# A decoder of two layers on one core: the slot order of the first stage, and the last step of the expert tiles

## The reference, cut to what matters

```python
x = x + L0_attn(layernorm(x))            # q, k, v each projected and layer-normed; softmax(k q^T) v, plus its own input
x = x + layernorm(x) * decayed_sum(ctx * ctx)     # r = 0.9 r + ctx^2 along the tokens
x = x + L0_ffn(layernorm(x))             # 8 experts, one per token, 1024 places each; tokens past that pass through
x = x + L1_attn(layernorm(x))            # 16 heads of 16
x = x + L1_xattn(layernorm(x), ctx)
x = x + L1_ffn(layernorm(x))             # the best 2 of 8 experts, weighted by their scores
```

## Time and profile before

| | before |
|---|---|
| median of 3 runs | 2639.61 us (2637.99 to 2640.75) |
| profiled execution: its own time | 2664.65 us |
| its span, first to last instruction | 2662.7 us |
| busy share of the span | PE 87%, PEld 69%, DVE 69%, ACT 60%, POOL 52% |
| first stage | 0 to about 540 us |
| experts of the last line | about 2357 us to the end |

### The profile page before, as it was taken

One profiled execution on the slowest core, in us unless ns is written; L12 is line 12 of the kernel. 1 busy time (PEld: TensorE's weight loads), 2 busy tenths in 40 slices (PEclk: granted clock), 3 DMA queues, 4 the chain that ended last, 5 costly groups with the idle time before them and its releaser, 6 DMA issues. The chain is left out here.

```text
span 2662.7 us, 49468 instructions
## 1 busy us (share of the span) xinstructions
PE 2303.4 (87%) x16108; PEld 1840.5 (69%) x16108; DVE 1840.6 (69%) x4594; ACT 1590.2 (60%) x3199; POOL 1377.3 (52%) x1384
## 2 busy tenths in 40 slices
PE   4888888659999957999999999988699999869987
PEld 4777777549988944565656565655588777659987
DVE  4777777645665536777777777775377777679877
ACT  4878778534655425676667676776244444348765
POOL 4777777544444245455445454541266666535554
PEclk9999999869999978999999999999799999879998
DMA  2222221162333110111111111111133333247574
GB/s 64 75 64 80 64 80 57 52 178 92 104 109 110 41 32 20 41 41 41 39 42 38 43 40 42 39 34 37 44 107 130 123 125 120 105 163 241 160 213 119
DMA packets 190220, 222.78 MB, mean 84 GB/s; under 512 B 36306, under 2 KB 166879, under 8 KB 189841
## 3 DMA queue, kind: packets, MB, share of 16 engines
q1 hardware_dynamic: 165008, 163.26, 20.8%
q0 software_dynamic: 23872, 56.37, 5.9%
q10 hardware_dynamic: 1088, 0.00, 0.0%
HBM read 128.15 MB, written 90.69 MB: 82 GB/s over the span
## 5 line engine op out<-in xcount | busy, mean ns | idle before, releaser
L1592 DVE TENSOR_REDUCE f_nm<-f_raw 128x4 f32<-128x1024 f32 x256 | 312.7, 1221 | 108.8 <-PE f_raw L1705 106.0
L1428 POOL TENSOR_TENSOR f_hm<-f_hm,f_mhalf 128x64 f32<-128x64 f32 x32 | 366.4, 11449 | 2.7
L1497 ACT ACTIVATE f_PT<-f_sco 128x1024 f32<-128x1024 f32 x256 | 262.3, 1025 | 96.4 <-PE f_sco L1722 96.2
L957 ACT ACTIVATE b_hT<-b_H,b_b1r 128x512 f32<-128x512 f32 x128 | 88.4, 691 | 162.6 <-PE b_H L1087 147.2
L1722 PE MATMUL f_sco<-f_q4T,f_k4T 64*128 64x256 f32 x1024 | 130.2, 334 | 49.8 <-DMA f_q4T<-f_nmT 35.6
L1102 PE MATMUL b_O<-b_w2l,b_hTh 128*128 128x256 f32 x512 | 144.9, 283 | 0.0
L1102 PE MATMUL b_O<-b_w2h,b_hTl 128*128 128x256 f32 x512 | 144.8, 283 | 0.0
L1102 PE MATMUL b_O<-b_w2h,b_hTh 128*128 128x256 f32 x512 | 144.7, 283 | 0.0
L910 POOL DMA_INDIRECT x_scratch<-b_y,b_idx x64 | 69.6, 1088 | 143.3 <-DVE b_y L1034 127.5
L1722 PEld LDWEIGHTS f_sco<-f_q4T,f_k4T 64*128 64x128 f32 x1024 | 81.9, 197 | 84.8 <-DMA f_q4T<-f_nmT 42.6
L1705 PE MATMUL f_raw<-f_k4T,f_q4T 64*128 64x256 f32 x1024 | 130.1, 334 | 7.3 <-DVE f_nm L1592 5.7
(11 more groups left out here) (406 smaller groups left out, 7905.3 us busy)
## 6 DMA issues: line engine op xcount, KB each, us to landing
x_scratch<-a_x SPq DMA_DIRECT2D x64, 256.0 KB, 2.2
b_w<-in_L_ffn_W_dram SPq DMA_DIRECT2D x16, 1024.0 KB
d_xs<-first_in SPq DMA_DIRECT2D x24, 544.0 KB
a_x<-in_x_dram SPq DMA_DIRECT2D x32, 256.0 KB
a_cx<-in_ctx_dram SPq DMA_DIRECT2D x32, 256.0 KB
f_x<-x_scratch SPq DMA_DIRECT2D x32, 256.0 KB
f_q4T<-f_nmT SPq DMA_DIRECT2D x128, 64.0 KB
f_xr<-x_scratch SPq DMA_DIRECT2D x32, 256.0 KB
```

The source lines that it names most:

```text
L957: s.activation(hT[f % 4][:, :], HB[f % 4][:, :], ACT.Gelu, bias=b1r[:, e, f:f + 1], scale=RATIO).then_inc(hidden, 1)
L1428: g.tensor_tensor(hm[b % 2][:, :], hm[b % 2][:, :], mhalf[:, :], ALU.pow).then_inc(hroot, 1)
L1497: s.activation(PT[n % 3][:, t, :, :], heads(SCO), ACT.Exp, scale=float(DH) ** -0.5).then_inc(probs_ready, 1)
L1592: v.tensor_reduce(nm[:, t, g * HG:(g + 1) * HG], heads(RAW), AX.X, ALU.max, negate=True)\
```

## The change

In the first stage `ORDER` is written anew. The squares of the context move from step "x2" (the first part of a slot) to step "sco" (behind the transposition "in T"), one slot sooner for a given row. The parts "in qk1" and "ln kT" change places. "pre stats" moves ahead of "sco inv" and "sco att", and "sco stats" moves to the end of the slot, behind "in v". In the experts `finish` runs two tiles late through nearly all of the second class (one tile late in four tiles near the end, and not late in the last four), where before it did so in the first four tiles of that class. The comparisons of `hide_seen` are done for all tiles at once before the first tile, and `load_part` takes the row number that the load of the same tile left in a register.

```diff
         ORDER = (
-            "x2 kv", "in norm", "route logits", "sco scores", "ln sq", "in T", "in low", "x2 sums", "x2 add",
-            "x2 stats", "sco exp", "route ranks", "in qk0", "ln scale", "sco prT", "ln kT", "in qk1", "x2 norm",
-            "sco inv", "sco att", "ln qT", "x2 T", "sco stats", "pre stats", "x2 pass", "in v")
+            "in norm", "route logits", "sco scores", "ln sq", "in T", "in low", "sco kv", "x2 sums", "x2 add",
+            "x2 stats", "sco exp", "route ranks", "in qk0", "ln scale", "sco prT", "in qk1", "ln kT", "x2 norm",
+            "pre stats", "sco inv", "sco att", "ln qT", "x2 T", "x2 pass", "in v", "sco stats")
...
-                   "sco exp": exps, "sco prT": take_prT, "x2 kv": square_ctx, "x2 norm": norm4, "x2 T": take_x2nT, "x2 pass": passed_by})
+                   "sco exp": exps, "sco prT": take_prT, "sco kv": square_ctx, "x2 norm": norm4, "x2 T": take_x2nT, "x2 pass": passed_by})
...
-        place, mask = sb("place", [P, T]), [sb(f"mask{n}", [P, T]) for n in range(ZR)]
+        place, hide = sb("place", [P, T]), [sb(f"hide{k}", [P, HALF - ex.WHOLE, T]) for k in range(2)]
...
-                ex.load_tile(sync, m)
+                row = ex.load_tile(sync, m)
+                if m >= HALF:
+                    row_of[m] = row
...
             def load_part(m):
-                row = sync.value_load(ex.row[0:1, m:m + 1], min_val=0, max_val=ex.spare)
+                row = row_of.pop(m)
...
             def hide_seen(m):
                 k = of_class(m)
-                if m == ex.WHOLE:
-                    dve.wait_ge(consts, 3)
-                n = m % HALF - ex.WHOLE
+                dve.wait_ge(masked, 2)
                 dve.wait_ge(scattered[(m - ZR) % XR], 16 * T * (turn(m - ZR) + 1))
-                v.tensor_scalar(mask[m % ZR][:, :], place[:, :], ex.over[k][:, n:n + 1], float(ex.OUT_OF_RANGE), ALU.is_lt, ALU.mult)\
-                    .then_inc(masked, 1)
-                masks[0] += 1
-                dve.wait_ge(masked, masks[0])
-                v.tensor_tensor(unseen[m % ZR][:, :], mask[m % ZR][:, :], targets(m), ALU.add)
+                v.tensor_tensor(unseen[m % ZR][:, :], hide[k][:, m % HALF - ex.WHOLE, :], targets(m), ALU.add)
...
+            dve.wait_ge(consts, 3)
+            for k in range(2):
+                v.tensor_tensor(hide[k][:, :, :], place[:, :].unsqueeze(1).broadcast_to([P, HALF - ex.WHOLE, T]),
+                                ex.over[k][:, :].unsqueeze(2).broadcast_to([P, HALF - ex.WHOLE, T]),
+                                ALU.is_lt).then_inc(covered, 1)
+            dve.wait_ge(covered, 2)
+            for k in range(2):
+                v.tensor_scalar(hide[k][:, :, :], hide[k][:, :, :], float(ex.OUT_OF_RANGE), None, ALU.mult).then_inc(masked, 1)
...
-                lag = LAG if HALF <= m < HALF + 4 else LAG // 2 if HALF <= m < HALF + 8 else 0
+                lag = LAG if HALF <= m < N - 8 else LAG // 2 if HALF <= m < N - 4 else 0
```

More of the change, by code:

```diff
@@ L1222, in load_tile @@
                        .rearrange("(p t) (k w) -> p t k w", p=P, w=self.W)).then_inc(self.xs_loaded[m % self.XR], 16)
+        return row
 def phase_c(nc, a, x3_d, out, w):
@@ L2366, in experts_phase @@
         out_psum, z_ready, finished = sem("out_psum"), sem("z_ready"), sem("finished")
-        masked = sem("masked")
+        covered, masked = sem("covered"), sem("masked")
         part_loaded, scattered = semn("part_loaded", XR), semn("scattered", XR)
@@ L2382, in _ @@
         def _(sync):
+            row_of = {}
             def load(m):
@@ L2492, in add_b2 @@
                                 b2[:, bass.ds(e, 1), :].broadcast_to([P, T, D]), ALU.add).then_inc(z_ready, 1)
-            masks = [0]
             def hide_seen(m):
                 k = of_class(m)
-                if m == ex.WHOLE:
-                    dve.wait_ge(consts, 3)
-                n = m % HALF - ex.WHOLE
+                dve.wait_ge(masked, 2)
                 dve.wait_ge(scattered[(m - ZR) % XR], 16 * T * (turn(m - ZR) + 1))
-                v.tensor_scalar(mask[m % ZR][:, :], place[:, :], ex.over[k][:, n:n + 1], float(ex.OUT_OF_RANGE), ALU.is_lt, ALU.mult)\
-                    .then_inc(masked, 1)
-                masks[0] += 1
-                dve.wait_ge(masked, masks[0])
-                v.tensor_tensor(unseen[m % ZR][:, :], mask[m % ZR][:, :], targets(m), ALU.add)
+                v.tensor_tensor(unseen[m % ZR][:, :], hide[k][:, m % HALF - ex.WHOLE, :], targets(m), ALU.add)
             def finish(m):
```

## The result

| | before | after |
|---|---|---|
| median of 3 runs | 2639.61 us | 2613.52 us (2610.29 to 2613.85) |
| ratio | | 0.9887, 95% interval 0.9869 to 0.9905 |
| profiled execution, span | 2662.7 us | 2611.5 us |

The kernel is 26.1 us faster by the two medians. 30.3 were forecast. The spans differ by 51.2 us, and the 25 us between the two numbers are the ones by which the profiled execution of before exceeded its median; they are taken up in the first experiment.

A forecast was written before the change was run, and what follows sets the result against it. A first-stage loop of waits, 6.62 us of DVE and 8.33 of POOL per 14.95 us slot, was taken as the bound. Terms -27.3 - 1.0 - 3.1 + 1.1 = -30.3 took 2639.6 to 2609.3 us; range 2603 to 2628.

The forecast's parts named there:

- The loop and its price: First stage: DVE and POOL waits set the 14.95 us slot; `rstd1` ahead of `root3` saves 1.01 us in 27 intervals, 27.3.
- the second chain: First stage: last value product on PE, `take_v`, `stats3`, then norm; about 0.3 us to spare, 0.1 to 0.2 after k's delay.
- The rival that gives part back: First-stage norm waits for `stats3` or partly for `root3`, losing 0.45 of 1.01 us per slot: 2621.5 us; chance 0.20.
- k's copy: ACT's copy of k begins near 261.2 instead of 260.14, so `norm4` begins 0.1 to 0.25 us later; cost nothing.
- The cover on POOL: First-stage POOL idle time: `root3` eats the 1.04 us before `rstd2`; the 1.40 us before `root4` stay.
- Norm beside `root3`: First stage: DVE's norm now runs while POOL does `root3` on 128x2; slowdown taken as nothing, other end 0.93 us per slot.
- The rival's 0.93 us: First-stage norm fully blocked by `root3`, losing 0.93 us per slot: 2634.4 us; chance 0.08, shared with any other whole loss.
- Fill and drain: Filling and emptying the first stage's pipeline: a gain of 1.0 us in all, 0 to 2.
- Masks and lag: Experts: masks done first gain 3.1 us over 28 tiles; late `finish` loses 1.1 us at the end, 0 to 2.6.
- The 25 us outside: Whole kernel: the 25.0 us between profiled execution and median before, left alike in the forecast.
- more than forecast: Rival in the experts: later `finish` relieves 22.9 us of waits that are really for scatters or loads: 2586 us; chance 0.05.
- The slower rival: First stage: late values on PE, as with a halved clock, make `stats3` set a longer slot: 2687 us; chance 0.05.

The follow-up runs named there:

- the first experiment: The kernel before, unchanged, profiled once more: this execution took 2648.3 us, tiles 39 to 66 took 91.96 us instead of 111.29.
- One move alone: Kernel before with only "pre stats" put ahead of "sco stats", both still ahead of the value sum: 2612.69 us, ratio 0.9895.

## Why the prediction was right, point by point

- **The loop and its price.** `rstd1` starts where `root3` did, the norm comes 1.01 us earlier: 0.99 measured in each slot, 26.7 us instead of 27.3. One move alone gives all of it, so the cause is shown, not only its sum.
- **What is late next.** `take_v` was to wait 1.2 us and the norm 0.3: they wait 1.16 and 0.38. That the second chain stands right behind is shown by the run with earlier statistics, in which it sets the slot. The rival that gives part back needed this chain to be some tenths later; k's copy, the term that was to bring it close, cost `norm4` 0.01 us. The cover on POOL came out otherwise than said: `root3` was to eat the 1.04 us before `rstd2` and leave the 1.40 before `root4`, and 0.55 and 0.88 are left. Both are still idle time, so nothing was lost by it.
- **Norm beside `root3`.** Nothing taken, nothing lost: 396/410/461 ns in the 64 rows of after. The rival's 0.93 us is real beside a 128x512 product (1.69 - 0.73 = 0.96 for the pair) and absent beside 128x2. The choice went by the earlier trace rows instead of the earlier trace rows, on the ground that `root3` works on 128x2. The instruction of the earlier trace rows is of another kind than the norm, but the run with the value sum ahead alone bears it out as a stand-in: L607 takes 0.17 us inside POOL's power of 128x6 and 1.21 beside its addition of 128x512. Whether the size of POOL's operand decides or the kind of its operation, no run separates.
- **Fill and drain.** The gain of 1.0 did not show. From the first norm to the fifth, that of the earlier trace rows at 73.64, the kernel before took 51.20 us (22.44 to 73.64), and the same order took 51.41 in the second profile of before and 52.80 with the experts alone; the new order took 51.95 (after), 51.90 (order alone) and 51.24 (old lag). The same order differs by up to 1.6 us from execution to execution, so neither a gain nor a loss can be told. The single move took 49.89, in one execution. From the last norm to the next stage's first work on DVE's line L1004 it was 87.3 us before and 87.0 after, where the two profiles of before differ by 0.1: as good as nothing.
- **Masks and lag.** Their sum, -2.0, is about what the trace gives (-2.3 + 0.4 = -1.9), but the terms were off and it is luck that they cancel: masks 2.3 instead of 3.1, and the late `finish` nothing instead of a cost of 1.1. Its tail alone cost 2.2 to 2.4, with 0.8 more in the steps before it. The prediction did not see that the old rule's catch-up in the second class costs steps (3.90 and 3.56 us instead of 3.29, twice: 1.8 us of the 3.0 that the lag spares), which pays for most of the tail.
- **The 25 us outside.** To leave them alike was right for the median; the second profile of before does not have its gaps in tiles 39 to 66. The rival "more than forecast" fell with them: the later `finish` relieved no wait, and where the earlier trace rows had 22.9 us of waits for PE the kernel after has 19.7, and the second profile of before 13.4.
- **The slower rival** did not come: the clock is 1.00 from 200 to 300 us, and `stats3` is in time. In the run with the value sum ahead alone the slots are longer and the clock is lower in part, but there the norm waits for `rstd1` behind `root3`, and its common slot is as long at a clock of 1.00. So no run shows this rival's mechanism.

By the trace's own terms: -26.7 for the slots, nothing that can be told for fill and drain, and -1.9 for the experts make -28.6, against 26.1 us by the medians and 29.8 (25.1 to 34.6) by the ratio. A closer test is not to be had: from the last norm to the first work of the experts, nearly all of it stages that no edit touches, the twelve profiles took from 1871 to 1884 us.

## What to carry to other kernels

Find the loop that sets the slot by going back from its wait to what releases it; then look on the releasing engine for work ahead of the release whose own reader comes late. Exchanging two such instructions was the whole gain here, and the spare time of the second-latest chain said beforehand how far the next step would reach. After each reordering read again which instructions of DVE and POOL now run side by side: a small cast or a norm beside a 128x512 operation of POOL cost up to 1 us, in one order 2 us in each slot.

## What the runs showed of the hardware

A DVE cast of 128x2 took 1.16 us instead of 0.17 beside POOL's 128x512 addition and ended with it, the norm's pair took 1.69 instead of 0.73 beside `gain_v`, and in one slot a `tensor_tensor` of 128x16 took 1.21 instead of 0.17. Beside POOL's addition and power of 128x2 and beside an indirect DMA the norm was not slowed, and a cast of 128x16 that began with POOL's power of 128x6 took 0.20 us instead of 0.17 (median of the run with one move). By the Trainium skill's rule (page "SBUF — State Buffer", section "Who interferes with whom") casts and `tensor_scalar` can enter a mode that takes a port pair shared with GpSimd, when their operands meet the conditions for it; whichever of the two engines issues first then keeps the pair for its whole instruction, and the other fully blocks. The trace agrees for POOL's 128x512 operands; beside its 128x2 operations, which last 0.21 and 0.72 us, it shows no block.
